# A second bank for q in the projection of an attention kernel, with the fourth score moved into the three score banks

## The chip, the cores and the metric

The kernel runs on one core of a Trainium2 chip. Its time is the device time of one launch in microseconds (us). Three runs of the kernel before took 796.98, 797.04 and 799.42 us; the median is 797.04 us.

## What is computed

One block of a transformer: x is (2, 512, 512), all in fp32. The part that the change touches is the attention's projection and its scores, cut here to what matters:

```
xn = layernorm(x)
q = rmsnorm((xn @ Wq.T) per head, q_norm_w)      # 32 heads of 128
k = rmsnorm((xn @ Wk.T) per head, k_norm_w)      # 8 heads of 128
v = (xn @ Wv.T) per head                         # 8 heads of 128
scores = q @ k.T / sqrt(128) + bias              # 4 q heads for each k head; causal, with slopes
attn = softmax(scores)
s = concat(attn @ v) @ Wo.T
g = silu(routed mixture of 8 rank-16 experts of xn)
out = x + s * g
```

## The kernel before, in words

The 1024 rows are 8 blocks of 128 (4 for each of 2 batches), and the 32 heads are 8 groups of 4 q heads with one k and one v head. One unit is one block of rows for one group: 64 units, numbered t. A unit of block i in its batch has i + 1 key blocks (`keys_of`), so 1, 2, 3, 4, 1, 2, 3, 4 over the 8 units of a group. Every fp32 product is made of three matmuls of split values, high x high, high x low and low x high (`three`, L1149 to L1153).

The five engines each run a list of their own, written out by hand, and meet by semaphores. In the steady part each list is a loop over slots (`slot`, once for each engine), 59 slots in all. In slot t:

- TensorE (PE) makes the scores of unit t, four heads; adds the output product of unit t - 3 (`out`); mixes the values of unit t - 2 (`mix`); and projects unit t + 3 (`project`): 4 chunks of the 512 input channels, and in each chunk 3 matmuls of 512 columns for q into one PSUM bank and 3 of 256 columns for k and v into a second (`qkv_ps`).
- VectorE (DVE) adds the bias to the scores (`bias`), sums the squares of q and k of unit t + 2 (`square_sums`), makes the low part of v, takes reciprocals, normalizes q and k of t + 2 in one instruction of 640 elements (`normalize_qk`, L963), transposes them in 32x32 squares (`square_both`), adds the output of t - 3, makes the low parts of q and k of t + 1 (`turned_qk_lo`), transposes the probabilities of t (`square_probs`) and makes the low part of the mix of t - 2 (`mixed_lo`).
- ScalarE (ACT) squares q and k of t + 2 in one instruction (`square_qk`, L678), copies v, takes the exponentials of t, then the high parts of q and k of t + 1 (`turned_qk_hi`, L664), scales the probabilities of t, and copies the moved probabilities of t - 1 (`moved_hi`, L691).
- GpSimd (POOL) makes the inverse root of the sums: an add of epsilon, a power and a product (`inverse_rms`, L517, L519, L523), and then the low parts of the moved probabilities of t - 1 (`turned_lo`, L529, one for each key block).
- The sync engine (SP) issues the transfers that finish the transposes through memory (`move`): 4 writes of the squared q and k of t + 2, 8 writes of the squared probabilities of t, 1 read of q and k, 2 reads of probabilities.

What holds the projection: the matmuls of unit t + 3 overwrite the two banks of `qkv_ps`, so they wait until v's low part and the normalization of unit t + 2 have read them:

```
if t > 0:
    pe.wait_ge(qk_norm_ready, ONE(g, t - 1, 1))
    pe.wait_ge(v_lo_ready, ONE(g, t - 1, 1))
```

Scores: heads 0, 1 and 2 go to three banks of `score_ps`, and from unit 3 on head 3 goes to `turn_ps`, so that PE writes all four scores of a unit without waiting for one of its biases (`score_bank`, `has_own_bank`). The bias of a head waits for its own score, except heads 2 and 3 together, and in units of 1 or 2 key blocks heads 0 and 1 together.

Memory: `squares` holds ACT's squares and then, under another name (`qk_squared`), the transposed q and k that SP's writes read. So ACT's squares of a unit wait for the writes of the unit before to have landed (`qk_written`, in `square_qk`).

Once in 8 slots (t = 5 of 8) the next group's projection weights are split as well, on ACT, DVE and POOL, and once (t = 2 of 8) the output weights, on ACT and POOL.

## Time and profile before

| | |
|---|---|
| median of three runs | 797.04 us |
| the profiled execution | 793.71 us |
| its span, first to last instruction | 791.6 us |
| mean granted TensorE clock over the span | 0.983 of full speed |
| busy: PE, PE weight load | 727.6 us (92%), 612.6 us (77%) |
| busy: DVE, ACT, POOL | 583.8 (74%), 559.6 (71%), 399.9 us (51%) |

Busy shares are means over stages. PE's matmuls overlap one another in the record (each lasts longer than the time to the next one's start), so PE's work is best read from start to start. What a wait costs is read where it stands: a gap in PE's row of starts is lost; a gap of another engine only where PE waits for it later.

### The profile page before, as it was taken

Reading aid. Unit: us, or ns where it says so; the run is one execution under the profiler, and the core shown is the slowest. Engines: PE = TensorE matmul, PEld = TensorE weight load, DVE = VectorE, ACT = ScalarE, POOL = GpSimd, SP = SyncE. Lnnn points to the kernel's source line nnn. Section 1 sums busy time; section 2 is a strip of 40 time slices with the busy share of each in tenths; the row PEclk is TensorE's granted clock in tenths of the full one; section 3 lists DMA queues with packets and bytes.
Section 4 is the critical chain, followed back from the end, with each engine's and each line's share of the span. In section 5 each row is a group of like instructions: output and inputs, shape, how many; then the busy total and the mean of one; then the engine's idle time right before and its main releaser. Section 6 shows DMA issues by size and latency. Waiting matters only on the chain.

```text
span 791.6 us, 14475 instructions
## 1 busy us (share of the span) xinstructions
PE 727.6 (92%) x3729; PEld 612.6 (77%) x3729; DVE 583.8 (74%) x1378; ACT 559.6 (71%) x1370; POOL 399.9 (51%) x423
## 2 busy tenths in 40 slices
PE   8888989999899999999899989999899998999697
PEld 7777867778788778887778778887787787787575
DVE  7855778677886778687877769778786778777555
ACT  4664767686676877777777876777686866768863
POOL 5313373555444762544644664445635554447347
PEclk9999999999999999999999999999999999999989
DMA  7014848678495767859485765858477784956642
GB/s 285 1 28 115 270 107 237 191 214 239 109 275 156 223 185 194 240 145 294 130 236 169 231 201 151 270 153 258 130 224 205 208 251 109 268 159 188 187 148 94
DMA packets 214772, 148.01 MB, mean 187 GB/s; under 512 B 48992, under 2 KB 205536, under 8 KB 214624
## 3 DMA queue, kind: packets, MB, share of 16 engines
q1 hardware_dynamic: 214752, 147.77, 64.7%
q8 instruction: 9, 0.15, 0.1%
q14 instruction: 11, 0.09, 0.0%
HBM read 85.84 MB, written 61.87 MB: 187 GB/s over the span
## 4 chain that ended last, share of the span: by engine, by line
PE 33%; issue 26%; POOL 24%; DVE 10%; ACT 4%; DMA 2%; POOLq 1%; SPq 1%; DVEq 0%; ACTq 0%
POOL pt_lo L529 10%; POOL inv_rms L519 8%; PE qkv_ps L1151 7%; PE qkv_ps L1152 6%; PE qkv_ps L1153 6%; POOL wo_lo L511 3%; DVE qk_norm L963 3%; DVE sums L947 2%; PE score_ps L1151 2%; PE score_ps L1153 2%; POOL sums_eps L517 2%; PE score_ps L1152 2%; PE out_ps L1151 2%; PE out_ps L1152 2%; PE out_ps L1153 2%
## 5 line engine op out<-in xcount | busy, mean ns | idle before, releaser
L529 POOL TENSOR_TENSOR pt_lo<-x_sb,pt_hi 128x512 fp32r<-128x512 f32 x153 | 195.3, 1303 | 240.8 <-ACT pt_hi L691 240.8
L1151 PE MATMUL qkv_ps<-w_hi,xt_hi 128*128 128x512 f32 (+1 forms) x512 | 182.0, 355 | 40.4 <-DVE qk_norm L963 38.4
L1152 PE MATMUL qkv_ps<-w_lo,xt_hi 128*128 128x512 f32 (+1 forms) x512 | 176.9, 345 | 0.0
L1153 PE MATMUL qkv_ps<-w_hi,xt_lo 128*128 128x512 f32 (+1 forms) x512 | 175.8, 343 | 0.0
L639 ACT ACTIVATE probs<-probs,neg_max 128x128 f32<-128x128 f32 (+3 forms) x256 | 141.7, 556 | 37.4 <-DVE neg_max L899 35.0
L1151 PEld LDWEIGHTS qkv_ps<-w_hi,xt_hi 128*128 128x128 f32 x512 | 99.2, 194 | 70.2 <-DVE qk_norm L963 34.6
L899 DVE CUSTOM_DVE_ANT_0 probs<-score_ps,cst,slope 128x128 f32<-128x128 f32 (+3 forms) x196 | 102.0, 545 | 54.1 <-PE score_ps L1153 46.1
L647 ACT ACTIVATE probs<-probs,recip 128x128 f32<-128x128 f32 (+3 forms) x252 | 122.2, 549 | 6.1 <-DVE recip L906 6.0
L918 DVE STREAM_TRANSPOSE squared<-probs 128x256 f32<-128x256 f32 (+3 forms) x124 | 99.7, 823 | 18.9 <-ACT probs L647 17.0
L1152 PEld LDWEIGHTS qkv_ps<-w_lo,xt_hi 128*128 128x128 f32 x512 | 99.6, 195 | 11.9
L1153 PEld LDWEIGHTS qkv_ps<-w_hi,xt_lo 128*128 128x128 f32 x512 | 99.2, 194 | 12.0
L963 DVE TENSOR_TENSOR qk_norm<-qkv_ps,inv 128x640 f32<-128x640 f32 x64 | 52.6, 822 | 71.5 <-POOL inv L523 71.5
L1151 PE MATMUL out_ps<-wo_hi,o_hi 128*128 128x512 f32 x252 | 100.4, 398 | 3.9 <-DVE o_lo L941 3.8
L1152 PE MATMUL out_ps<-wo_lo,o_hi 128*128 128x512 f32 x252 | 98.8, 392 | 0.0
L1153 PE MATMUL out_ps<-wo_hi,o_lo 128*128 128x512 f32 x252 | 98.7, 392 | 0.0
L691 ACT ACTIVATE pt_hi<-x_sb 128x512 fp32r<-128x512 f32 x153 | 86.0, 619 | 13.9 <-DMA x_sb<-turning 13.8
L678 ACT ACTIVATE squares<-qkv_ps 128x640 f32<-128x640 f32 x64 | 44.7, 698 | 65.0 <-PE qkv_ps L1153 54.4
L519 POOL TENSOR_TENSOR inv_rms<-sums_eps,minus_half 128x5 f32<-128x5 f32 x64 | 78.5, 1227 | 5.0
L664 ACT ACTIVATE q_hi<-qk_moved 128x512 fp32r<-128x512 f32 x45 | 28.4, 630 | 68.0 <-DMA qk_moved<-turning_qk 68.0
L947 DVE TENSOR_REDUCE sums<-squares 128x5 f32<-128x640 f32 x64 | 52.3, 818 | 22.0 <-ACT squares L678 21.7
L1151 PE MATMUL mix_ps<-pt_hi,v_hi 128*128 128x512 f32 x160 | 62.6, 391 | 0.0
L1153 PE MATMUL mix_ps<-pt_hi,v_lo 128*128 128x512 f32 x160 | 62.3, 389 | 0.0
(166 smaller groups left out, 1444.7 us busy)
## 6 DMA issues: line engine op xcount, KB each, us to landing
turning_qk<-squares SPq DMA_DIRECT2D x240, 80.0 KB, 1.9
qk_moved<-turning_qk SPq DMA_DIRECT2D x60, 320.0 KB, 3.2
turning<-squared SPq DMA_DIRECT2D x120, 128.0 KB, 2.2
x_sb<-turning SPq DMA_DIRECT2D x30, 512.0 KB, 5.0
w_raw<-wqkv SPq DMA_DIRECT2D x32, 384.0 KB, 5.3
turning<-squared SPq DMA_DIRECT2D x120, 96.0 KB, 1.9
x_sb<-turning SPq DMA_DIRECT2D x30, 384.0 KB, 4.2
turning<-squared SPq DMA_DIRECT2D x128, 64.0 KB, 1.8
```

The costliest lines, as they stand in the source:

```text
L519: nc.gpsimd.tensor_tensor(inv_rms[:, :], sums_eps[:, :], minus_half[:, 0:NORMED], ALU.pow).then_inc(inv_rms_ready, 1)
L529: nc.gpsimd.tensor_tensor(by_quad(pt_lo, j), moved_block(t, j), by_quad(pt_hi, j).bitcast(F32), ALU.subtract).then_inc(pt_lo_by_pool, 1)
L639: nc.scalar.activation(probs[:, h, 0:n], probs[:, h, 0:n], ACT.Exp, bias=neg_max[:, h:h + 1], scale=-1.0, accum_out=total[:, h:h + 1]).the ...
L647: nc.scalar.activation(to[:, h, 0:n], probs[:, h, 0:n], ACT.Copy, scale=recip[:, h:h + 1]).then_inc(probs_ready, 1)
L691: nc.scalar.activation(by_quad(pt_hi, j), moved_block(t, j), ACT.Copy).then_inc(pt_hi_ready, 1)
L899: nc.vector.tensor_tensor_reduce(probs[:, h, 0:n], score_bank(t, h, at_end), cst[:, C_DIST + SEQ - n:C_DIST + SEQ], slope[:, h:h + 1], HUG ...
L918: nc.vector.transpose(blocks[:, :, 0:keys_of(t), :, :], probs[:, h:h + 2, 0:n].rearrange("p h (j k n) -> p h j k n", k=QUADS, n=QUAD)).the ...
L947: nc.vector.tensor_reduce(sums[:, :], squares[:, :].rearrange("p (h d) -> p h d", h=NORMED), AX.X, ALU.add).then_inc(sums_ready, 1)
L963: nc.vector.tensor_tensor(qk_norm[:, :, :], qkv_flat[:, 0:QK].rearrange("p (h d) -> p h d", h=NORMED), inv[:, :].unsqueeze(2).broadcast_to ...
L1151: pe.matmul(out, a_hi, b_hi, start=start, stop=False)
L1152: pe.matmul(out, a_hi, b_lo, start=False, stop=False)
L1153: return pe.matmul(out, a_lo, b_hi, start=False, stop=stop)
```

## The change

- The projection's q has two banks by turns, from unit 6 on (`two_banks`): `turn_ps` for even units and the first bank of `qkv_ps` for odd ones. q's 12 matmuls come before the 12 of k and v. q waits for the normalization of q of two units before (`q_norm_ready`), k and v for that of k of the unit before and for v's low part. Where the weights are new (block 0 of a group) the order is q, q, kv, kv of the first two chunks, then q, kv, q, kv.
- Head 3's score gives up `turn_ps`. In units of 1 or 2 key blocks it takes the free half of the third score bank. In units of 3 or 4 key blocks it takes head 0's bank, and waits for head 0's bias.
- The biases wait by twos in all units from 3 on: head 0's waits for the scores of heads 0 and 1.
- ACT squares q (512 elements) and k (128) by two instructions, DVE normalizes k (128) and q (512) by two; the reciprocals of heads 2 and 3 come between them.
- The normalized q and k now lie in the memory of the squares, and the transposed ones in memory of their own. So ACT's squares wait for DVE's transpose of the unit before, and DVE's transpose waits for the writes of the unit before.
- Each row of squares has one more element, which holds the epsilon, so the sum has it in and POOL's add is gone.

The diff, its core:

```
+        squares = sb("squares", [NORMED, HD + 1])
+        qk_norm = squares[:, :, 0:HD]
-        qk_squared = squares[:, :].rearrange("p (k n) -> p k n", k=QUADS)
+        qk_squared = sb("qk_squared", [QUADS, NORMED * QUAD])
...
+        def q_ps(u):
+            return turn_ps[:, :] if two_banks(u) and u % 2 == 0 else qkv_ps[:, 0, :]
+        def two_banks(u):
+            return u >= BY_TURN + 2
...
-        def score_bank(t, h, at_end=False):
+        def score_bank(t, h):
             n = keys_of(t) * P
-            if h == 3 and has_own_bank(t, at_end):
-                return turn_ps[:, 0:n]
+            if h == 3 and has_half(t):
+                return score_ps[:, 2, SEQ // 2:SEQ // 2 + n]
             return score_ps[:, h % (3 if t >= 2 else 2), 0:n]
+        def has_half(t):
+            return t >= 2 and keys_of(t) <= 2
...
 POOL, inverse_rms
-                nc.gpsimd.tensor_tensor(sums_eps[:, :], sums[:, :], eps_sum[:, :], ALU.add).then_inc(eps_added, 1)
-                pool.wait_ge(eps_added, ONE(g, u, 1))
...
 ACT, square_qk
-                act.wait_ge(qkv_ready, ONE(g, u, 1))
-                if u > BY_TURN:
-                    act.wait_ge(qk_written, QK_WRITTEN(g, u - BY_TURN, 0))
-                nc.scalar.activation(squares[:, :], qkv_flat[:, 0:QK],
+                act.wait_ge(q_ready, ONE(g, u, 1))
+                if 0 < u <= BY_TURN:
+                    act.wait_ge(qk_turned, TWO(g, u, 0))
+                elif u > BY_TURN:
+                    act.wait_ge(qk_squared_ready, ONE(g, u - BY_TURN, 0))
+                nc.scalar.activation(squares[:, 0:HPG, 0:HD], q_ps(u).rearrange("p (h d) -> p h d", h=HPG),
                                      ACT.Square).then_inc(squares_ready, 1)
+                act.wait_ge(kv_ready, ONE(g, u, 1))
+                nc.scalar.activation(squares[:, HPG, 0:HD], k_ps, ACT.Square).then_inc(squares_ready, 1)
...
 DVE, bias
-                by_twos = t > 2 and not at_end and (h >= 2 or keys_of(t) <= 2)
+                by_twos = t > 2 and not at_end
...
 DVE, square_both
-                dve.wait_ge(qk_norm_ready, ONE(g, u, 1))
+                dve.wait_ge(q_norm_ready, ONE(g, u, 1))
+                if u > BY_TURN:
+                    dve.wait_ge(qk_written, QK_WRITTEN(g, u - BY_TURN, 0))
...
 DVE, slot
-                    normalize_qk(g, t + 2)
+                    normalize_k(g, t + 2)
...
                     reciprocals(g, t, 2)
                 if here(t + 2, left):
+                    normalize_q(g, t + 2)
                     square_both(g, t + 2)
...
 PE, project_q and project_kv
+                if c == 0:
+                    if two_banks(t):
+                        pe.wait_ge(q_norm_ready, ONE(g, t - 2, 1))
+                    elif t > 0:
+                        pe.wait_ge(q_norm_ready, ONE(g, t - 1, 1))
...
+                if c == 0 and t > 0:
+                    pe.wait_ge(k_norm_ready, ONE(g, t - 1, 1))
+                    pe.wait_ge(v_lo_ready, ONE(g, t - 1, 1))
...
+                if two_banks(t) and t % BLOCKS > 0:
+                    for c in chunks:
+                        project_q(g, t, c)
+                    for c in chunks:
+                        project_kv(g, t, c)
...
 PE, scores
-                elif h == 3 and not has_own_bank(t, at_end):
+                elif h == 3 and not has_half(t):
                     pe.wait_ge(biased_ready, PER_HEAD(g, t, 1))
```

How the rows stand now. PE, the end of the scores of a unit of 4 key blocks, before and then in the change (`score_ps` are the three score banks, `turn_ps` the bank that head 3 had; in brackets the semaphores waited for):

```order
L1151 MATMUL score_ps<-k_hi,q_hi 128x512
L1152 MATMUL score_ps<-k_lo,q_hi 128x512
L1153 MATMUL score_ps<-k_hi,q_lo 128x512
L1151 MATMUL turn_ps<-k_hi,q_hi 128x512
L1152 MATMUL turn_ps<-k_lo,q_hi 128x512
L1153 MATMUL turn_ps<-k_hi,q_lo 128x512
L1308 ISA
L1312 ISA [waits acc_ready,o_lo_ready]
```

```order
L1170 MATMUL score_ps<-k_hi,q_hi 128x512
L1171 MATMUL score_ps<-k_lo,q_hi 128x512
L1172 MATMUL score_ps<-k_hi,q_lo 128x512
L1303 REGISTER_ALU
L1170 MATMUL score_ps<-k_hi,q_hi 128x512 [waits biased_ready]
L1171 MATMUL score_ps<-k_lo,q_hi 128x512
L1172 MATMUL score_ps<-k_hi,q_lo 128x512
L1358 ISA
L1362 ISA [waits acc_ready,o_lo_ready]
```

Head 3 had no wait, and now has one for head 0's bias in the middle of the scores.

PE, the start of the projection in the same slot, before and then in the change:

```order
L1161 REGISTER_ALU
L1151 MATMUL qkv_ps<-w_hi,xt_hi 128x512 [waits v_lo_ready,qk_norm_ready]
L1152 MATMUL qkv_ps<-w_lo,xt_hi 128x512
L1153 MATMUL qkv_ps<-w_hi,xt_lo 128x512
L1151 MATMUL qkv_ps<-w_hi,xt_hi 128x256
L1152 MATMUL qkv_ps<-w_lo,xt_hi 128x256
```

```order
L1180 REGISTER_ALU
L1170 MATMUL turn_ps<-w_hi,xt_hi 128x512 [waits q_norm_ready]
L1171 MATMUL turn_ps<-w_lo,xt_hi 128x512
...
L1200 REGISTER_ALU
L1170 MATMUL qkv_ps<-w_hi,xt_hi 128x256 [waits v_lo_ready,k_norm_ready]
L1171 MATMUL qkv_ps<-w_lo,xt_hi 128x256
L1172 MATMUL qkv_ps<-w_hi,xt_lo 128x256
```

The wait for the unit before has moved behind q's 12 matmuls; in front of them stands a wait for the unit two before.

DVE, from v's low part to the transpose of q and k in one slot, before and then in the change (`squares` is now also the name of the memory of the normalized q and k):

```order
L953 TENSOR_TENSOR v_lo<-qkv_ps,v_hi 128x128 [waits v_hi_ready]
L906 RECIPROCAL recip<-total 128x2 [waits exp_ready]
L963 TENSOR_TENSOR qk_norm<-qkv_ps,inv 128x640 [waits qk_squared_ready,inv_ready]
L906 RECIPROCAL recip<-total 128x2 [waits exp_ready]
L969 STREAM_TRANSPOSE squares<-qk_norm 128x5x4x32 [waits qk_norm_ready]
```

```order
L964 TENSOR_TENSOR v_lo<-qkv_ps,v_hi 128x128 [waits v_hi_ready]
L915 RECIPROCAL recip<-total 128x2 [waits exp_ready]
L969 TENSOR_TENSOR squares<-qkv_ps,inv 128x128 [waits inv_ready]
L915 RECIPROCAL recip<-total 128x2 [waits exp_ready]
L974 TENSOR_TENSOR squares<-turn_ps,inv 128x4x128
L982 REGISTER_ALU [waits q_norm_ready]
L983 STREAM_TRANSPOSE qk_squared<-squares 128x5x4x32 [waits qk_written]
```

k is normalized first, by itself; q's normalization comes after the second reciprocal, and the wait for the writes stands at the transpose.

## Rows read from the trace of the kernel before

**Rows 1.** The page: busy time of each engine.

```profile
PE 727.6 (92%) x3729; PEld 612.6 (77%) x3729; DVE 583.8 (74%) x1378; ACT 559.6 (71%) x1370; POOL 399.9 (51%) x423
```

**Rows 2.** Waits: who waited for whom, us in total, times, longest.

```profile
DVE qk_norm L963 <- POOL inv L523: 71.5, 55, 2.6
ACT q_hi L664 <- DMA qk_moved<-turning_qk: 68.0, 36, 3.5
ACT squares L678 <- PE qkv_ps L1153: 54.4, 24, 5.5
...
PE qkv_ps L1151 <- DVE qk_norm L963: 38.4, 29, 3.0
...
ACT squares L678 <- DMA turning_qk<-squares: 10.0, 11, 2.0
```

**Rows 3.** Windows, projections alone: stretch, its length, PE busy, granted clock, DMA.

```profile
107.46:113.30 5.84, 5.84 (x24) 0.71 0.23 56
...
656.62:661.22 4.60, 4.45 (x24) 1.00 0.29 71
541.13:545.43 4.30, 4.30 (x24) 1.00 0.71 221
```

**Rows 4.** Windows, one group of 8 slots: length, busy PE, PEld, DVE, ACT, POOL, clock.

```profile
463.90:555.30 91.40, 86.48 (x438) 72.80 (x437) 70.03 (x162) 67.26 (x166) 47.76 (x50) 0.98 0.70 200
```

**Rows 5.** Timeline of PE: start, duration, what, idle before it and releaser.

```profile
107.46 0.49 PE L1151 MATMUL qkv_ps<-w_hi,xt_hi 128*128 128x512 f32 x1 [2.96 <-DVE qk_norm L963]
```

**Rows 6.** Timeline of PE, scores of 4 key blocks: the first matmuls of heads 2, 3.

```profile
399.05 0.39 PE L1151 MATMUL score_ps<-k_hi,q_hi 128*128 128x512 f32 x1
...
399.73 0.39 PE L1151 MATMUL turn_ps<-k_hi,q_hi 128*128 128x512 f32 x1
```

**Rows 7.** Timeline of DVE: head 0's bias in the same unit.

```profile
398.81 0.73 DVE L899 CUSTOM_DVE_ANT_0 probs<-score_ps,cst,slope 128x512 f32<-128x512 f32 x1
```

**Rows 8.** Timeline, the same slot: from one transfer of q and k to the next.

```profile
404.23 0.63 ACT L664 ACTIVATE x_sb<-qk_moved 128x512 f32<-128x512 f32 x1 [1.05 <-DMA qk_moved<-turning_qk]
...
406.79 2.47 DVE L918 STREAM_TRANSPOSE squared<-probs 128x1024 f32<-128x1024 f32 x2 [0.96 <-ACT probs L647]
...
415.81 0.63 ACT L664 ACTIVATE q_hi<-qk_moved 128x512 fp32r<-128x512 f32 x1 [2.08 <-DMA qk_moved<-turning_qk]
```

**Rows 9.** Timeline of ACT: squares of 640 elements, then v's high part of 128.

```profile
377.36 0.71 ACT L678 ACTIVATE squares<-qkv_ps 128x640 f32<-128x640 f32 x1 [1.65 <-DMA turning_qk<-squares]
377.96 0.27 ACT L683 ACTIVATE v_hi<-qkv_ps 128x128 fp32r<-128x128 f32 x1
378.11 0.85 ACT L594 ACTIVATE w_hi<-w_raw 128x768 fp32r<-128x768 f32 x1
```

**Rows 10.** Timeline of ACT: 512 elements from PSUM, and what starts behind them.

```profile
352.00 0.57 ACT L653 ACTIVATE o_hi<-mix_ps 128x512 fp32r<-128x512 f32 x1
352.48 1.14 ACT L691 ACTIVATE pt_hi<-x_sb 128x512 fp32r<-128x512 f32 x2
```

**Rows 11.** Timeline of DVE: 128, 640 and 512 elements from PSUM, each with its successor.

```profile
345.28 0.29 DVE L953 TENSOR_TENSOR v_lo<-qkv_ps,v_hi 128x128 fp32r<-128x128 f32 x1
345.48 0.16 DVE L906 RECIPROCAL recip<-total 128x2 f32<-128x2 f32 x1
346.12 0.82 DVE L963 TENSOR_TENSOR qk_norm<-qkv_ps,inv 128x640 f32<-128x640 f32 x1 [0.48 <-POOL inv L523]
346.86 0.15 DVE L906 RECIPROCAL recip<-total 128x2 f32<-128x2 f32 x1
...
347.74 0.65 DVE L988 TENSOR_TENSOR acc<-out_ps,acc 128x512 f32<-128x512 f32 x1
348.32 0.67 DVE L929 TENSOR_TENSOR q_lo<-qk_moved,q_hi 128x512 fp32r<-128x512 f32 x1
```

**Rows 12.** Lines by form, POOL: epsilon's add, mean ns in front of the bar's idle time.

```profile
L517 POOL TENSOR_TENSOR sums_eps<-sums,eps_sum 128x5 f32<-128x5 f32 x64 | 17.2, 269 | 87.4 <-DVE sums L947 87.4
```

**Rows 13.** Timeline of POOL: the same add beside DVE's split of the weights.

```profile
469.79 0.93 POOL L517 TENSOR_TENSOR sums_eps<-sums,eps_sum 128x5 f32<-128x5 f32 x1
```

More of the change, by code:

```diff
@@ L944, in square_sums @@
             def square_sums(g, u):
[L946 to L947 removed]
+                dve.wait_ge(squares_ready, TWO(g, u, 2))
+                if u == 0:
+                    dve.wait_ge(eps_set, 1)
+                nc.vector.tensor_reduce(sums[:, :], squares[:, :, :], AX.X, ALU.add).then_inc(sums_ready, 1)
             def value_lo(g, u):
@@ L1177, in project @@
-                if KC - 1 in chunks:
-                    last.then_inc(qkv_ready, 1)
+                if t == 0:
+                    pe.wait_ge(w_lo_done, c + 1)
+                elif m == 0 and c < EARLY_W:
+                    pe.wait_ge(w_lo_by_dve, (g + t // BLOCKS - 1) * EARLY_W + (c + 1))
+                elif m == 0:
+                    pe.wait_ge(w_lo_by_pool, (g + t // BLOCKS - 1) * (KC - EARLY_W) + (c - EARLY_W + 1))
+                last = three(q_ps(t), xt_hi[:, c, rows], xt_lo[:, c, rows], w_hi[:, c, 0:QW], w_lo[:, c, 0:QW], c == 0, c == KC - 1)
@@ new lines, in project_q, with project_kv @@
+                if c == KC - 1:
+                    last.then_inc(q_ready, 1)
+            def project_kv(g, t, c):
+                m = t % BLOCKS
+                rows = slice(m * P, (m + 1) * P)
+                if c == 0 and t > 0:
+                    pe.wait_ge(k_norm_ready, ONE(g, t - 1, 1))
+                    pe.wait_ge(v_lo_ready, ONE(g, t - 1, 1))
+                last = three(qkv_ps[:, 1, 0:QKV - QW], xt_hi[:, c, rows], xt_lo[:, c, rows],
+                             w_hi[:, c, QW:QKV], w_lo[:, c, QW:QKV], c == 0, c == KC - 1)
+                if m == BLOCKS - 1 and c < EARLY_W:
+                    last.then_inc(w_left, 1)
+                if c == KC - 1:
+                    last.then_inc(kv_ready, 1)
@@ L1346, in end @@
                 for h in range(3):
-                    scores(g, last, h, at_end=True)
+                    scores(g, last, h)
                 mix(g, before - 1, 1)
@@ L1350, in end @@
                     turn_probs(before, n)
-                scores(g, last, 3, at_end=True)
+                scores(g, last, 3)
                 out(g, before - 1)
```

97 lines of the change are left out of this document (45 added, 52 removed).

## The prediction

> **What bounds the kernel now.** I read the busy times first: PE is busy 92% of the span, so what it loses is small and has to be found place by place [rows 1]. The view of waits gives the place: PE waited 38.4 us in 29 pieces for DVE's normalization before a projection [rows 2]. The timeline of PE shows the worst kind, 2.96 us idle before the first matmul at 107.46 [rows 5]. Such a wait costs twice: that projection had a mean granted clock of 0.71 and took 5.84 us, against 4.30 us at clock 1.00 elsewhere [rows 3]; so PE ran a part of it at the lower of its two levels, 1.2 GHz instead of 2.4.
>
> But PE is not alone. ACT waited 68.0 us in 36 pieces for the transfer of q and k, DVE 71.5 us in 55 pieces for POOL's inverse, and ACT only 54.4 us in 24 pieces for PE's projection [rows 2]. So there is a second ring without PE in it: ACT takes q and k (404.23), scales the probabilities, DVE transposes them (406.79, 2.47 us), SP issues 8 writes and then the read of q and k, and ACT takes the next q and k on landing, at 415.81: 11.58 us for a slot of 4 key blocks, with a wait at both ends [rows 8]. A group of 8 slots takes 91.4 us, in which PE is busy 86.5 [rows 4]. The reader is to see two rings of nearly equal length; a change that shortens one is paid only as far as the other follows.
>
> **The change, part by part.** There are 59 steady slots, or 7.4 groups of 8.
>
> *q's second bank, kv behind q.* PE's wait now stands behind q's 12 matmuls, which are 12 x 0.228 = 2.7 us (three take 399.73 - 399.05 = 0.68 us [rows 6]), and needs only k's normalization, which ends some 0.5 us earlier than the joint one (0.20 against 0.74 us from start to start [rows 11]). The longest wait is 3.0 us [rows 2], so cover of 3.2 us swallows all of them. Of the 38.4 us about 3.6 lie in front of units below 6, which keep one bank; 34.8 go. Seven projections took longer than 4.5 us, the first and the last of them in [rows 3]; above 4.30 they cost 1.5 us each in four cases and 1.3, 0.3 and 0.3 us in the others, 8 us in all. PE's side: **-43 us** as a ceiling. What is late next is the first score of the next unit, which waits for q and k of the other ring.
>
> *Head 3 in head 0's bank.* It touches 30 slots, 15 of 4 and 15 of 3 key blocks. Head 3 would start 0.68 us after head 2 [rows 6]. It now waits for head 0's bias: this starts when head 1's last matmul is out, 399.05 + 0.16 (the record's 0.39 less the 0.23 to the next start), plus about 0.2 for the signal, takes 0.73 [rows 7], and about 0.2 for its accumulator and the way back: 400.3 against 399.73, so 0.6 us. If DVE comes late, by the 0.3 us that a longer queue before the bias easily gives, 0.9. Bounds: 30 x 0.6 = 18 and 30 x 0.9 = 27 us; nothing below, since no row lets the bias end before head 2's matmuls. I take 0.67, **+20 us**, near the lower end, because in [rows 7] DVE begins its bias at 398.81, before the second score is out. Queued behind that wait on PE: the output, the mix and the projection. PE's side nets -23.
>
> *Biases by twos.* DVE's first bias waits for head 1 as well, 0.68 us later. It costs where DVE waits for PE; it is inside the 0.6 above. The exponentials behind it have ACT's later wait for q and k as cover (1.9 us on the mean, 68.0 / 36 [rows 2]); without that cover it would be 0.68 us a slot.
>
> *Two squares and two normalizations for one each.* By starts: ACT's 640 elements hold it 0.60 us, 128 hold it 0.15 [rows 9], 512 hold it 0.48 [rows 10], so +0.03. DVE: 0.74, 0.20 and 0.58 [rows 11], so +0.04. With 59 slots: **+4 us** in the second ring. q's squares can start before k and v are projected, which is worth up to 0.45 us in the slots where ACT waits for PE, 24 of 64 [rows 2]: **-7 us** at 0.3 each.
> By durations the split would cost more: 0.57 + 0.27 - 0.71 on ACT [rows 9, 10] and 0.65 + 0.29 - 0.82 on DVE [rows 11], together 0.25 us a slot, 15 us in all. The Trainium skill (VectorE: DVE Perf Modes, "The TRN2 errata") gives a fixed part for each instruction that reads PSUM, 172 cycles on ScalarE and 120 on VectorE; from it I estimate 0.27 us a slot, 16 us in all, as the durations have it and unlike the starts. I go by the starts, because the next instruction of the same engine does begin before the record of the one before it ends [rows 9, 11].
>
> *The squares' memory.* ACT's wait for the writes, 10.0 us in 11 pieces [rows 2], goes; DVE's transpose, which comes later, gets it, with about 4 us more room in between. **-10 us** in the second ring as a ceiling, nothing as a floor (where ACT only reaches its next wait sooner); I take 8.
>
> *POOL's add.* 0.27 us on the mean [rows 12], in the path where DVE waits for the inverse (55 of 64 slots [rows 2]), but in the ring of ACT and the transfers only where the normalization holds DVE's transposes, which I put at 3 slots in 8: 0.27 x 22 = **-6 us**. Beside the weights' split it took 0.93 us [rows 13]; the mean has this in it, and I add nothing for it.
> The Trainium skill (SBUF — State Buffer, "shared port pair") says that a GpSimd instruction that reads SBUF and a VectorE one with two SBUF inputs exclude one another for their whole length. By that the power takes over the add's 0.7 us of blocking, and the sum gets nothing extra from those 7 slots; counting the 0.93 as saved would give 5 us more.
>
> **The sum.** PE's ring: -43 + 20 = -23. Second ring: +4 - 7 - 8 - 6 = -17, of which I take off 1 for the reciprocals that now stand in front of q's normalization. Both must be shorter for the time to be; the lesser is 16. The profiled execution took 793.7 us and so comes to 777.7; the median is 3.3 above it, and 797.0 - 16 gives **781 us**. From no change one can tell here about 0.3%, 2.4 us.
>
> **The rivals.**
> 1. *PE leads and the second ring follows* (its waits were only idle time before a late PE). For it: 24 waits of ACT for PE [rows 2]. Against it: q and k arrive late in more slots. Then PE's side with head 3 at its lower bound is paid, -43 + 18 = -25: 772 us.
> 2. *The second ring doesn't shorten.* If the split instructions cost their durations, 15 instead of 4 us, the ring gives -17 + 11 = -6: 791 us, and with the wait for the writes moved rather than gone, -6 + 8 = +2: 799. PE's waits would then stand at the first score or the output instead of the projection. This holds too if the second bank does not do what it says. For it: ACT and DVE are busy 71% and 74% of the span with waits in every slot [rows 1, 2]. Against it: the starts of [rows 9 to 11]. Centre 793.
> 3. *Slower: head 3's wait.* Place: PE, in the middle of the scores of units with 3 or 4 key blocks. DVE does its transposes (2.47 us for 4 key blocks [rows 8]) and the mix's low part before the first bias. If PE, with its waits gone, comes to the scores that much earlier, head 3 waits for all of DVE's arrears: up to 2.1 us for 4 key blocks and 1.1 for 3, which is 15 x 3.2 = 48 us against the 43 won; with the +4 of the splits 797 + 9 = 806. It decides from 43 / 30 = 1.4 us a slot on. For it: DVE had no idle time before the bias in [rows 7]. Against it: it was not late there.
>
> **How the numbers follow.** The forecast has 0.52, rival 1 0.13, rival 2 0.19 (half of it below 794.6 and half within 0.3%), rival 3 0.16. Faster is 0.52 + 0.13 + 0.09 = 0.74, the same 0.10, slower 0.16. The range goes from 768 (rival 1 with 4 us for the bound of the other terms) to 799 (the end of rival 2), and leaves rival 3 out.
>
> **What would show it.** PE's wait for a normalization before a projection under 5 us in total, and no projection at a clock below 0.9 behind one; a new wait of head 3's score for a bias, 30 times, 12 to 27 us by the view of waits; ACT's wait for the writes gone, and DVE's transpose without one; ACT's wait for the transfer of q and k as large as now or larger; waits of PE at the first score for the low part of k. The forecast is wrong if head 3's waits are over 1.4 us each, if ACT's wait for q and k shrinks while PE has none (rival 1), or if a group of 8 slots still takes 91 us (rival 2).

## The result, and the profile of the changed kernel

The changed kernel takes **823.3 us** (median of 4, 819.8 to 826.1) against 797.0 for the kernel before in the same session: ratio 1.030, interval 1.026 to 1.033, slower. The prediction was 781 us with a range of 768 to 799; the time lies outside it, on the other side. The profiled execution took 819.8 us. Here and below medians are of all runs, and ratios with their 95% intervals are of the runs in the faster of the chip's two states.

The page of the changed kernel, span and busy times, then the two queues that fetch instructions (packets, MB, share of 16 engines):

```profile
span 818.0 us, 14522 instructions
...
PE 736.7 (90%) x3729; PEld 617.1 (75%) x3729; DVE 604.2 (74%) x1442; ACT 562.8 (69%) x1434; POOL 388.5 (47%) x359
...
q14 instruction: 42, 0.34, 0.1%
q8 instruction: 9, 0.15, 0.1%
```

PE is busy 9 us longer than in [rows 1] and idle 17 us longer. The q14 line is new. The kernel before had the line below; packets and bytes of the other queues are the same in both.

```profile
q14 instruction: 11, 0.09, 0.0%
```

The waits of the changed kernel (who waited for whom: us in total, times, longest), to be held against [rows 2]:

```profile
ACT probs L643 <- DVE neg_max L908: 88.2, 88, 3.3
ACT q_hi L668 <- DMA qk_moved<-turning_qk: 80.3, 36, 3.8
...
DVE squares L969 <- POOL inv L527: 47.8, 46, 2.4
PE score_ps L1170 <- DVE neg_max L908: 42.6, 29, 5.3
...
DVE probs L908 <- issue: 24.4, 13, 5.7
...
PE score_ps L1170 <- DVE k_lo L942: 15.4, 11, 7.7
...
PE qkv_ps L1170 <- DVE squares L974: 3.4, 2, 2.4
```

Much of what the prediction said one would see is there: the wait before the projection fell from 38.4 to 3.4 us, ACT's wait for the writes is gone, its wait for q and k grew from 68.0 to 80.3, PE waits at the first score for the low part of k. Three things are not as foreseen. A group of 8 slots takes 95.5 us, not less than 91 (columns as in [rows 4]), which is the prediction's own sign for a second ring that does not shorten:

```profile
462.30:557.80 95.50, 87.55 (x436) 73.18 (x436) 72.70 (x171) 67.72 (x174) 46.28 (x43) 0.98 0.68 192
```

Head 3's wait is 42.6 us, and DVE stands idle for 24.4 us with no releaser at all ("issue"). The timeline of DVE and PE shows that the last two meet at the first slot of a pass of the loop (start, duration, what, idle time before it):

```profile
363.55 0.69 DVE L950 TENSOR_TENSOR o_lo<-mix_ps,o_hi 128x512 fp32r<-128x512 f32 x1 [0.45 <-ACT o_hi L657]
367.04 0.75 DVE L908 CUSTOM_DVE_ANT_0 probs<-score_ps,cst,slope 128x512 f32<-128x512 f32 x1 [2.81 <-issue]
```

```profile
361.57 0.39 PE L1170 MATMUL score_ps<-k_hi,q_hi 128*128 128x512 f32 x1
...
367.86 0.80 PE L1170 MATMUL score_ps<-k_hi,q_hi 128*128 128x512 f32 x1 [4.76 <-DVE neg_max L908]
368.45 0.63 PE L1171 MATMUL score_ps<-k_lo,q_hi 128*128 128x512 f32 x1
```

The scores that the bias needs were out by 362.2 (the first line of PE is head 1's first matmul), DVE was free at 364.2, and its bias began at 367.0. PE waited 4.76 us in the middle of the scores and then ran matmuls of 0.63 us instead of 0.39. This comes back six times, once in each later pass of 8 slots, with 2.7 to 2.9 us of DVE's idle time and a wait of 4.6 to 5.3 us on PE each. In the other slots head 3's wait is 0.4 to 0.7 us, but for one of 1.2 and one of 1.7. Of the 24.4 us another 5.7 stand once, ahead of the loop.

### The profile page after: what moved, and what is told of

The parts are those of the page before. It is cut to its first block, busy times and chain, and to the rows that moved or that the text cites. A ratio compares the mean times of both kernels' runs of the same rounds, so it can differ in the third digit from the quotient of the medians.

```text
span 818.0 us, 14522 instructions
## 1 busy us (share of the span) xinstructions
PE 736.7 (90%) x3729; PEld 617.1 (75%) x3729; DVE 604.2 (74%) x1442; ACT 562.8 (69%) x1434; POOL 388.5 (47%) x359
## 4 chain that ended last, share of the span: by engine, by line
issue 33%; POOL 13%; DVE 11%; DMA 10%; ACT 9%; SPq 9%; PE 7%; DVEq 0%; ACTq 0%; POOLq 0%
SPq L433 9%; DMA qk_moved<-turning_qk 8%; POOL pt_lo L533 7%; POOL inv_rms L523 5%; ACT probs L651 4%; DVE squared L927 3%; DVE k_lo L942 2%; DVE probs L908 1%; DVE q_lo L938 1%; ACT wo_hi L608 1%; ACT probs L643 1%; DVE sums L958 1%; POOL inv L527 1%; DMA w_raw<-wqkv 1%; PE score_ps L1170 1%
## 5 line engine op out<-in xcount | busy, mean ns | idle before, releaser
L908 DVE CUSTOM_DVE_ANT_0 probs<-score_ps,cst,slope 128x128 f32<-128x128 f32 (+3 forms) x256 | 130.0, 544 | 71.1 <-PE score_ps L1172 32.9
L1170 PE MATMUL qkv_ps<-w_hi,xt_hi 128*128 128x256 f32 (+1 forms) x396 | 128.6, 325 | 5.4 <-DVE squares L974 3.4
L1171 PE MATMUL qkv_ps<-w_lo,xt_hi 128*128 128x256 f32 (+1 forms) x396 | 127.9, 323 | 0.0
L1172 PE MATMUL qkv_ps<-w_hi,xt_lo 128*128 128x256 f32 (+1 forms) x396 | 127.4, 322 | 0.0
L523 POOL TENSOR_TENSOR inv_rms<-sums,minus_half 128x5 f32<-128x5 f32 x64 | 78.5, 1227 | 98.8 <-DVE sums L958 98.8
L1170 PE MATMUL score_ps<-k_hi,q_hi 128*128 128x256 f32 (+2 forms) x192 | 71.6, 373 | 58.2 <-DVE neg_max L908 42.6
L1170 PEld LDWEIGHTS score_ps<-k_hi,q_hi 128*128 128x128 f32 x192 | 37.1, 193 | 73.9 <-DVE neg_max L908 53.9
L668 ACT ACTIVATE q_hi<-qk_moved 128x512 fp32r<-128x512 f32 x45 | 28.4, 631 | 80.3 <-DMA qk_moved<-turning_qk 80.3
L1171 PE MATMUL score_ps<-k_lo,q_hi 128*128 128x256 f32 (+2 forms) x192 | 66.8, 348 | 0.0
L1172 PE MATMUL score_ps<-k_hi,q_lo 128*128 128x256 f32 (+2 forms) x192 | 66.8, 348 | 0.0
L958 DVE TENSOR_REDUCE sums<-squares 128x5 f32<-128x645 f32 x64 | 52.6, 822 | 15.4 <-ACT squares L688 15.3
```

Source lines behind the costliest of these rows:

```text
L523: nc.gpsimd.tensor_tensor(inv_rms[:, :], sums[:, :], minus_half[:, 0:NORMED], ALU.pow).then_inc(inv_rms_ready, 1)
L908: nc.vector.tensor_tensor_reduce(probs[:, h, 0:n], score_bank(t, h), cst[:, C_DIST + SEQ - n:C_DIST + SEQ], slope[:, h:h + 1], HUGE, ALU.a ...
L958: nc.vector.tensor_reduce(sums[:, :], squares[:, :, :], AX.X, ALU.add).then_inc(sums_ready, 1)
L1170: pe.matmul(out, a_hi, b_hi, start=start, stop=False)
L1171: pe.matmul(out, a_hi, b_lo, start=False, stop=False)
L1172: return pe.matmul(out, a_lo, b_hi, start=False, stop=stop)
```

## The experiments

**Theories.** *Code position:* the change added instructions on VectorE; its loop now ends at instruction 394 of its program instead of 382 and has passed the edge of a block of instruction memory. *Theory 1:* head 3's wait and the split pieces are slow by themselves, on TensorE's path. *Theory 2:* the second ring, through SyncE and the transfers, sets the slot, and PE only waits elsewhere. *Theory 3:* the second bank does give time, and the split pieces take it back. Ratios are to the kernel before in the same session (797.3 to 800.2 us).

### Position in the code

```
# 1 and 2, kernel before, DVE, ahead of its loop (n = 12, 4)
+            for _ in range(n):
+                dve.engine_nop()
```

> The kernel before with 12 empty instructions on VectorE in front of its loop, so that the loop ends at instruction 394 of VectorE's program, where the changed kernel's loop ends, instead of 382. Nothing else differs. Theory (code position): the loop's last instructions have passed the edge of a block of instruction memory, so that each jump back to the loop's start waits for code: VectorE idles 2 to 4 us with no releaser at the start of each of its 6 or 7 later loop passes, TensorE waits there, and the time is 820 to 840 us, with some 40 packets in the instruction queue instead of 11. Rival (head 3's wait and the split pieces are slow by themselves): 12 empty instructions of about 0.06 us cost under 1 us once, 797 to 798 us, 11 packets.

> The kernel before with 4 empty instructions on VectorE in front of its loop: the loop ends at 386. Theory (code position): either the edge is not passed yet and the time stays 797 us, or it is passed and the time is 820 to 840 as with 12; nothing between. Rival: 797 us.

With 12 empty instructions the kernel before takes **819.1 us** (1.027, 1.022 to 1.032), with 4 of them 797.8 (0.999, 0.996 to 1.003). The page and the waits of the run with 12:

```profile
q14 instruction: 42, 0.34, 0.2%
```

```profile
DVE probs L899 <- issue: 17.1, 6, 3.2
...
DVE sums L947 <- issue: 10.7, 6, 2.1
```

Twice in each later pass DVE stands for code, about 2.9 and 1.8 us on the mean. PE pays before the projection, where it waits 56.7 us for the normalization instead of 38.4. The 31 further packets carry 0.25 MB. So 21 us hang on where a loop lies.

The Trainium skill (Runtime: NRT & Kernel Launch, "Instruction fetch mechanics") says that code is fetched in blocks of 256 instructions, that two blocks are held, fetched in sequence, and that a taken branch out of them stalls. The trace agrees on the extra fetches at each jump back. That two blocks are held it does not show: this loop, of some 240 to 250 instructions, touches only two blocks and stalls all the same.

```
# 3, changed kernel: 244 x dve.engine_nop() behind VectorE's first memsets
# 4, changed kernel, "trimmed"
-            normalize_k(0, 0)
-            normalize_q(0, 0)
+            normalize_qk(0, 0)                 # units 0 to 3
...
+            with dve.Fori(0, GROUPS - 1) as g:
+                for t in range(3, BLOCKS + 3):
+                    tail(g, t - 1, GROUPS)     # square_probs x2, mixed_lo
+                    slot(g, t, GROUPS)
...
```

> The changed kernel with 244 empty instructions on VectorE at the front of its program: the loop's body, itself unchanged, stands at 393 to 638 and so within one block of 256 instructions again if the edge lies between 382 and 394. Theory (code position): the idle time without a releaser at the loop's start goes (6 times 2.7 to 2.9 us), TensorE's wait for head 3's bank in the first slot of a pass falls from about 5 to about 1 us, one group of heads takes 88 to 90 us instead of 95, and the time is 823 - 38 plus what 244 empty instructions cost at the front, up to 15 us: 785 to 800. Rival: the waits in the first slot stay at 5 us, 823 plus 5 to 15 us: 828 to 838.

> The changed kernel with 9 instructions fewer on VectorE ahead of the loop's end: the first four units are normalized by one instruction each, the loop is turned so that the transposes of the probabilities and the subtraction of the slot before stand at its top, the first memsets are joined or on POOL, and the first square signals nothing of its own. The loop is at 140 to 385. Theory (code position): if the edge lies at 385 or later (the second run tells: it holds for 386), the time is 779 to 790 us, and the loop's start shows no idle time without a releaser; if it lies at 382 to 384, the time stays 818 to 826. Rival: 820 to 826 whatever the edge, since the score banks' waits are unchanged.

Both take the stall away (13 and 11 packets), by moving the same loop or by shortening what stands before it. The first measured 824.2 us, outside both of its forecasts. It has 8.4 us of idle time at its front, where the empty instructions stand, and the 5.7 once ahead of the loop, which the changed kernel has too and the trimmed one has not; since they stay when the code moves by 244 instructions, they do not hang on this edge. Its later passes take 93.2 us on the mean (from jump to jump of VectorE), those of the trimmed kernel 93.4, those of the changed kernel 95.0; so in the steady part the two agree, and 8.4 + 5.7 us cover what they differ by. The trimmed kernel takes **812.8 us** (1.020, 1.014 to 1.026) against 823.3: 10 us of the changed kernel's 26 are code position, 8 by the ratios. The forecast 779 to 790 was wrong: 15 us remain. Its waits on PE:

```profile
PE score_ps L1182 <- DVE neg_max L909: 22.4, 29, 2.1
PE score_ps L1182 <- DVE k_lo L943: 15.9, 11, 7.7
PE turn_ps L1182 <- POOL w_lo L508: 5.3, 12, 0.5
```

and a group of 8 slots (its columns as in [rows 4]):

```profile
472.00:565.00 93.00, 87.31 (x443) 72.62 (x442) 72.57 (x171) 67.48 (x174) 47.02 (x42) 1.00 0.69 195
```

Head 3's wait is now 22.4 us in 29 pieces. That looks like the predicted 20 (bounds 18 to 27), but it is made of two things. 21 of the waits are 0.4 us on the mean, 8.3 us together. The other 8 are 1.2 to 2.1 us, 14.1 us together, seven of them at the same slot of a group, and DVE has no idle time without a releaser there. Here is one, from the trimmed kernel's timeline:

```profile
357.28 0.98 DVE L928 STREAM_TRANSPOSE squared<-probs 128x768 f32<-128x768 f32 x1 [1.08 <-ACT probs L653]
358.70 0.69 DVE L951 TENSOR_TENSOR o_lo<-mix_ps,o_hi 128x512 fp32r<-128x512 f32 x1 [0.44 <-ACT o_hi L659]
359.31 0.74 DVE L909 CUSTOM_DVE_ANT_0 probs<-score_ps,cst,slope 128x512 f32<-128x512 f32 x1
360.11 0.50 PE L1182 MATMUL score_ps<-k_hi,q_hi 128*128 128x512 f32 x1 [1.77 <-DVE neg_max L909]
```

PE had come early, and DVE still had the transpose and the low part of the mix of the slot before to do: the mechanism of the prediction's rival 3, in one slot of eight. Of the changed kernel's waits of 4.6 to 5.3 us some 2.8 are the code, and about 2 are this.

All runs below are built on this one or on the kernel before, and all but the eighth show 11 or 12 packets.

### The parts one by one

> The kernel before with the change's score part alone: head 3 takes head 0's bank (a half of head 2's bank for one or two key blocks) and all biases wait by twos; one bank for q, joint normalization, the add on POOL and the shared memory as before. VectorE's loop ends at 378. Theory 1 (head 3's wait is a price on TensorE's path): TensorE's waits at the first score matmul of head 3 come in as 22 us in 29 places, as in the trimmed changed kernel, its waits before the projection stay above 30 us, and the time is 810 to 820. Theory 2 (a ring through VectorE and ScalarE sets the slot, TensorE only waits elsewhere): the projection's waits fall from 38 by about what head 3's waits add, 797 to 803.

> The kernel before with the eps as a column of the squares (POOL's add is gone, some 0.3 us of 1.2 in each unit), the normalization in the squares' memory and the turned squares in memory of their own; joint normalization, banks and biases as before. VectorE's loop ends at 384. My terms for these parts, 6 us for the add and 0 to 8 for the memory: 783 to 793, with TensorE's wait before the projection at 25 to 32 instead of 38. Rival (the inverse is not on the path that sets the slot): 796 to 799, and VectorE waits as before.

```
# 5, kernel before: score part alone
-            if h == 3 and has_own_bank(t, at_end):
-                return turn_ps[:, 0:n]
+            if h == 3 and has_half(t):
+                return score_ps[:, 2, SEQ // 2:SEQ // 2 + n]
# 6, kernel before: epsilon as a column of squares, no add on POOL,
#    norms in the squares' memory, qk_squared apart
```

The score part takes 802.5 us (1.007, 1.005 to 1.009), the memory part 800.8 (1.002, 0.999 to 1.005). In the first, the waits are

```profile
PE qkv_ps L1151 <- DVE qk_norm L963: 30.4, 24, 2.8
PE score_ps L1151 <- DVE neg_max L899: 11.6, 29, 0.6
```

so head 3 brings 11.6 us (0.4 a slot) and the projection gives 8 of it back: theory 2 for this part. The 14 us that the prediction had for the memory and the add did not come. The two together:

> The kernel before with the score part and the memory part of the change together (head 3 in head 0's bank, biases by twos, no add on POOL, the normalization in the squares' memory), joint squares and joint normalization, one bank for q. VectorE's loop ends at 380. Against the run of the trimmed kernel without the second bank (824) only the split pieces, q's and k/v's matmuls in that order, and the trimming are missing. If the split is what costs (theory 3): 801 to 809, the sum of the two parts alone (5 and 3 us). If the two parts cost more together than apart: 815 to 826.

801.7 us against 800.2 (1.002, 1.000 to 1.005). These parts are nearly free.

> The trimmed changed kernel with head 3's score matmuls on TensorE behind the first head's three output matmuls (0.7 us) instead of ahead of them, so that the wait for head 0's bias has something in front of it. Theory 1: the waits for head 0's bias fall from 22 to under 5 us, and the time from 813 to 793 to 800. Theory 2 (the ring sets the slot, and head 3's scores now come up to 0.7 us later for VectorE): 810 to 820, and the waits come back at the projection or at the first score.

```
# 7, PE, trimmed kernel
+                    for h in range(3):
+                        scores(g, t, h)
+                if here(t - 3, left):
+                    out(g, t - 3, range(0, 1))
+                if here(t, left):
+                    scores(g, t, 3)
+                if here(t - 3, left):
+                    out(g, t - 3, range(1, HPG))
```

812.7 us: no change. Head 3's wait is gone from the list, and this stands in its place:

```profile
PE out_ps L1182 <- DVE o_lo L951: 17.1, 20, 1.8
...
PE out_ps L1182 <- POOL wo_lo L519: 11.7, 6, 2.3
```

Taking 22 us of waits from PE gave nothing, and they came back at the output. That fits theory 2, by which PE's path is not what sets the time while all transfers are in place. It does not prove it, since the edit also gives VectorE head 3's scores up to 0.7 us later.

> The trimmed changed kernel with the score banks of before (head 3 in its own bank, the biases of heads 0 and 1 apart for three and four key blocks) and one bank for q; what is left of the change is k and q normalized and squared apart, q's matmuls in front of k's and v's by chunks, and the squares' memory. VectorE's loop ends at 389: whether the edge is passed shows in the instruction queue (11 packets or about 42). Theory 1: without head 3's wait and without the second bank the split pieces cost 1 to 4 us net of the memory's gain: 795 to 802. Theory 2 (the split itself, 0.29 and 0.68 us in place of 0.82 and 0.25 us more on ScalarE, lengthens the ring): 808 to 815. With 42 packets 10 to 20 us more in either.

> The trimmed changed kernel without the second bank for q (every unit's q in the first bank); the score banks, the biases by twos, the split normalization and squares, q's matmuls in front of k's and v's chunk by chunk and the squares' memory as in the change. VectorE's loop ends at 385. If the second bank gives nothing because a ring through SyncE and the transfers sets the slot (theory 2): 811 to 818, no more than 4 us from the 813 with it, and TensorE's waits before the projection are back at 25 to 40 us. If the second bank does give time and the split pieces take it away again (theory 3): 825 to 845.

```
# 12, trimmed kernel (8: also the score banks of before)
         def two_banks(u):
-            return u >= BY_TURN + 2
+            return False
```

The eighth shows 42 packets and so says nothing on the split (829.3 us); with the second it puts the edge between 386 and 389. The twelfth takes 823.9 us (814.9 to 828.1; 1.027, 1.019 to 1.035). The forecasts were 811 to 818 without a worth of the bank and 825 to 845 with one, and the time lies between. The second bank thus gives about 11 us by the medians and 5 by the ratios, and the intervals overlap (1.019 to 1.026). Against the run with joint squares below, whose interval lies clear of the trimmed kernel's, it is 9 by the ratios: a gain, of a size that stays open. What is left, 20 to 25 us over the run with the score and memory parts, lies in the split, the order of q's and k/v's matmuls and the trimming; the two runs that follow tell them apart.

> The trimmed changed kernel without the second bank, with q's and k's squares in one instruction (0.70 us, instead of 0.59 and 0.27), k and q still normalized apart. If the second square, 0.15 us later for the sums, is the larger part of the split's price: 808 to 816. If it is the split normalization (q's end comes behind a reciprocal, and TensorE's next q waits for it): 818 to 826.

> The trimmed changed kernel without the second bank, with q's normalization directly behind k's, ahead of the second reciprocal (0.15 us) instead of behind it; nothing else differs from the run without the second bank (824). From the start of the first normalization to the end of the last it took 1.18 us a unit there against 0.82 in the kernel before. If that end is what the split costs on the projection's path: 1.18 falls by 0.1 to 0.2 us, and the time by 6 to 14 us, to 810 to 818. If the order of q's and k/v's matmuls or the trimming is what costs: 821 to 827.

```
# 17, ACT, on 12: one Square over 640 columns
# 18, DVE, on 12
                 if here(t + 2, left):
                     normalize_k(g, t + 2)
+                    normalize_q(g, t + 2)
                 if (t + 3) % BLOCKS == 0 and here(t + 3, left):
                     set_factor(g, t + 3)
                 if here(t, left):
                     reciprocals(g, t, 2)
                 if here(t + 2, left):
-                    normalize_q(g, t + 2)
                     square_both(g, t + 2)
```

Joint squares: 824.3 us (1.031, 1.028 to 1.034), so the second square costs nothing. q's normalization directly behind k's: **804.2 us** (1.006, 1.004 to 1.009), 20 us less for one instruction moved (16 to 20 by the ratios), more than the 6 to 14 expected. The order of the matmuls and the trimming are still in this run, so together with the two instructions they cost at most some 3 us over the score and memory parts. The timeline of VectorE shows why, first of the run without the second bank, then with the instruction moved:

```profile
393.91 0.29 DVE L976 TENSOR_TENSOR squares<-qkv_ps,inv 128x128 f32<-128x128 f32 x1 [1.06 <-POOL inv L529]
394.12 1.54 DVE L896 COPY factor<-cst 128x5 f32 x1
395.58 0.15 DVE L916 RECIPROCAL recip<-total 128x2 f32<-128x2 f32 x1
395.65 0.67 DVE L981 TENSOR_TENSOR squares<-qkv_ps,inv 128x512 f32<-128x512 f32 x1
```

```profile
387.43 0.29 DVE L976 TENSOR_TENSOR squares<-qkv_ps,inv 128x128 f32<-128x128 f32 x1 [1.06 <-POOL inv L529]
387.64 0.68 DVE L981 TENSOR_TENSOR squares<-qkv_ps,inv 128x512 f32<-128x512 f32 x1
388.24 0.96 DVE L896 COPY factor<-cst 128x5 f32 x1
```

The change had put not only the reciprocals of heads 2 and 3 in front of q's normalization, but in one slot of each group the copy of the factors too, which takes 1.54 us there. It began 0.29 us behind this on POOL, and in all seven groups it ended about 0.03 us after the first of the two instructions (393.83 to 395.63 here):

```profile
393.83 3.58 POOL L508 TENSOR_TENSOR w_lo<-w_raw,w_hi 128x768 fp32r<-128x768 f32 x2
```

From the start of the first normalization to the end of the last a unit takes 0.82 us before, 1.18 in the run without the bank and 0.89 with the instruction moved (means over 60 units of VectorE's timeline). Seven units of the 60, those with the copy, take 2.4 us each in the second. Times 60, 0.30 us are 18 us, near the 20 that were won, and more than half of them lie in the units with the copy. PE paid for it right away, at 396.45, and more in matmuls at the slower clock, of 0.63 us instead of 0.39:

```profile
396.45 0.79 PE L1182 MATMUL qkv_ps<-w_hi,xt_hi 128*128 128x512 f32 x1 [3.65 <-DVE squares L981]
397.03 0.63 PE L1183 MATMUL qkv_ps<-w_lo,xt_hi 128*128 128x512 f32 x1
```

PE's waits for q's normalization, without the second bank and then with the instruction moved:

```profile
PE qkv_ps L1182 <- DVE squares L981: 34.3, 20, 3.7
```

```profile
PE qkv_ps L1182 <- DVE squares L981: 22.7, 20, 2.2
```

They differ by 11.6 us. PE's busy time (744.2 and 739.4 us) and head 3's wait (15.7 and 11.3 us) add 9, which makes 21 us, against 19 between the two spans (821.6 and 802.4 us).

The slots also show what the second bank did. From ScalarE's copy of one unit's transferred q to that of the second unit after it, the pair of slots that begins with the copy of the factors takes 26.6 us without the bank, 24.5 with it (the trimmed kernel), 24.4 without it but with the instruction moved, and 24.2 in the run with the score and memory parts alone (means of five groups). So in these slots the bank and the moved instruction take away the same 2.2 us a group, 16 us in all: the bank mostly gave back what the late q had cost. That it gives anything beyond this no run shows.

### Transfers

> The kernel before with one step of SyncE's order moved: the read of the next unit's turned q and k is issued behind the first pair's four probability writes instead of behind all eight (a write's issue takes 0.46 us on SyncE, so 1.9 us earlier). Nothing is added or removed. Theory 2 (a ring sets the slot: q and k land, ScalarE's q_hi and k_hi and probabilities, VectorE's transpose of the probabilities, SyncE's writes and the next read, landing): ScalarE's wait for q and k falls from 68 to 10 to 40 us, TensorE's wait before the projection grows or stays, and the time is 770 to 790, since TensorE's 728 busy us stand next. Theory 1 (TensorE with the normalization sets it): 795 to 799, and ScalarE waits for something else.

> The trimmed changed kernel with the same step of SyncE's order moved. Theory 2: the second bank for q can now pay, so this gains more than the kernel before does from the same move: from 813 to 765 to 785, with TensorE's waits for the projection under 5 us and head 3's waits at 12 to 25. Theory 1: 808 to 815. If it gains only as much as the kernel before (20 us or less) and stays above it, head 3's wait and the split pieces cost more than the second bank gives even without the ring.

> The same with head 3's score matmuls behind the first head's output matmuls. Theory 2: with the ring loose, head 3's wait lies on TensorE's path, so hiding it is worth 5 to 20 us against the run before it, where it was worth nothing with the ring tight. If the ring still binds: no difference within 3 us.

```
# 9, 10 (11: also 7), SyncE, behind the first pair's writes instead of behind both
-                if u is not None:
-                    sp.wait_ge(qk_written, ...)
-                    sp.dma_start(qk_moved[:, :, :], ...)
+                    if u is not None and pair == 0:
+                        sp.wait_ge(qk_written, QK_WRITTEN(g, u - BY_TURN, 16 * QUADS))
+                        sp.dma_start(qk_moved[:, :, :], turning_qk[u % 2, ...])
```

The forecasts failed: 832.1 us from the kernel before, 817.2 from the trimmed one, 814.0 with head 3 late as well. Waits of ScalarE in the run from the kernel before:

```profile
ACT pt_hi L691 <- DMA x_sb<-turning: 74.0, 29, 6.1
...
ACT q_hi L664 <- DMA qk_moved<-turning_qk: 12.8, 16, 1.6
```

q and k were hardly waited for any more (68.0 us before), but the probabilities came late instead (13.8 before), since SyncE stood 47.9 us for the writes of q and k with the second pair's writes behind it. The move bought one transfer with another. With this order the trimmed kernel is the faster of the two, by 15 us (11 by the ratios), but both are slower than the kernel before.

> The kernel before with half of what is turned through DRAM left out: of the probabilities and of q and k only two of four quarters are written and read back (so the other half of their turned values is stale), which takes half of SyncE's issues (0.46 us each) and half of the bytes out of the slot. Theory 2 (transfers and their issue set the slot): 745 to 785, ScalarE's waits for q and k under 20 us, and TensorE's waits for the normalization stay or grow. Theory 1: 790 to 799.

> The trimmed changed kernel with the same half of the turned values left out. Theory 2: with the transfers out of the way the second bank pays, and this is 5 to 25 us faster than the kernel before with half of its moves, while with all moves it is 15 us slower. Theory 3 (head 3's wait and the split pieces cost more than the second bank gives under any transfers): slower than it by 5 to 20 us.

> The same with head 3's score matmuls behind the first head's output matmuls. If head 3's wait lies on TensorE's path once the transfers are out of the way: 5 to 20 us faster than the run before it. Otherwise within 3 us of it.

```
# 13 to 15, SyncE: both writes and both reads
-                    for q in range(QUADS):
+                    for q in range(HALF):
```

With half of the turned values left out the kernel before takes **748.9 us** (0.937, 0.934 to 0.941), the trimmed one 759.7, and 754.4 with head 3 late. So the transfers and their issue hold 48 us of the kernel before: theory 2's ring is real. PE is then busy 96% of the span, and its wait before the projection is

```profile
PE qkv_ps L1153 <- DVE qk_norm L965: 13.3, 16, 2.4
```

Theory 2 had expected this wait to stay or to grow. It fell from 38.4 us with nothing changed on PE or VectorE, so 25 us of what the second bank was to win were waits that the transfers had caused further up. The second bank has little left to win here; the trimmed kernel is 11 us slower than the kernel before, as theory 3 had it, and now, unlike with all transfers, hiding head 3's wait is worth 5 us.

## Why the prediction was wrong

**q's second bank, -43 as a ceiling, -23 paid after head 3.** The mechanism was right in part: the waits before the projection went. The granted clock of the profiled run did not rise, 0.975 against 0.983 before, and 0.985 in the trimmed kernel. The worth was wrong: 5 to 11 us against a run in which q is late, and by the slots above mostly a repair of that lateness. 25 of the 38.4 us were the transfers' doing (run 13). The prediction did name the other ring and took the lesser of two sums; but the gains that it gave the second ring did not come (below), and of the waits that were taken from PE a part came back at k's low part (15.9 us against 6.8 before) and the weights' low part (5.3 against 0.6).

**Head 3 in head 0's bank, +20.** As a sum the wait was near (22.4 us in the trimmed kernel), and that was in part luck. The plain wait is 0.4 us of idle time a slot, or nearly 0.6 from start to start, since a matmul's record lasts 0.16 us beyond the next one's start; so the 0.6 of the prediction's lower bound holds, though no row had shown its two terms of 0.2 us. The rest are eight long waits, for DVE's arrears. As a price it was 5 us alone and 2 with the memory part. A wait on PE is not a price when another ring sets the slot. Rival 3 wanted its arrears in every such slot; they came in one slot of eight, at 1.2 to 2.1 us. Its sign, over 1.4 us each, did come (42.6 us in 29 pieces), but only because DVE's waits for code stood on top.

**Split squares and normalizations, "+4 us", and 1 us for the reciprocals.** This is the step that failed most. The squares cost nothing, as costed by starts. The late end of q's normalization cost 16 to 20 us where q has one bank (runs 12 and 18): it went from 0.82 to 1.18 us behind the start of the first. The prediction costed the two instructions (+0.04) and put 1 us for the reciprocals in between, and did not list the copy of the factors, which the change had put there too and which takes 1.5 us beside POOL's split of the weights. The 15 or 16 us that the prediction set against the starts, from durations and from the fixed part in the Trainium skill (VectorE: DVE Perf Modes, "The TRN2 errata"), came nearer in size, but for another reason: with q directly behind k, two instructions end 0.07 us later than one, nearer to the +0.04 of the starts than to the +0.12 of the durations. What the late q costs with two banks was not measured by itself.

**The squares' memory -8, the add -6, q's squares earlier -7.** Memory and add together measured +1.5 us (interval -1 to +4). ACT's 10.0 us of waits for the writes went and gave no time. Its waits for PE before the squares fell from 54.4 to 21.6 us in the trimmed kernel, which no run has by itself. VectorE's gap from the end of the sums to the start of the normalization fell by only 0.12 us (2.64 to 2.52 in run 16), not 0.27, without the add. So the second ring, forecast 18 us shorter, did not shorten: a group takes 93.4 us in the trimmed kernel, 91.2 in the kernel before. That is the mechanism of rival 2, which had it end at 799 at most.

**What no step had.** The length of VectorE's loop. Nothing in the prediction counts instructions against the place of the code; the order of the changed kernel's instructions would have shown the loop's end move by 12. It is worth 8 to 10 us here, and 21 in the kernel before.

In sum, from the kernel before: score and memory parts +2, the split with q late about +22, the second bank -5 to -11, code position +8 to +10. The last two are uncertain by some 6 to 8 us to both sides, and the sum holds for this order of steps only, since the split's price and the bank's gain are in part the same time.

**Open.** The obvious kernel, second bank with q's normalization directly behind k's and the loop inside a block, was not run. If the gains of the bank and of the moved instruction added, it would come to about 793 to 799; the slots above speak against that, since both take away the same 2.2 us a group. So a time nearer to run 18's 804 is as likely, and no gain over the kernel before is to be expected from what was measured. Where the 15 us that the trimmed kernel keeps over the kernel before go, slot by slot, stays open too. No kernel that was run and does the whole computation beats the kernel before.

## What to carry to other kernels

Where an instruction is split, cost the end of the last piece, with everything that the new order lets in between, and not the pieces. A wait that vanishes from one engine is worth something only if this engine sets the slot; a run with something else taken away (half of the transfers, here) shows how much of the wait was that other thing's. And count the instructions of an engine's loop: when a change moves its end or start, look at the packets of the instruction queue before explaining any wait.

## What the runs showed of the hardware

- A loop of some 240 to 250 instructions on VectorE that ends at 389 or 394 of its program has 31 packets of code more over the run and stands 2.6 to 3.9 us once in each later pass, in the run with 12 empty instructions also 1.4 to 2.1 us a second time. One that ends at 386, or lies at 393 to 638, has no such stop in its passes. The edge lies between 386 and 389 of the kernel's own instructions.
- Empty instructions are not free: 244 of them at the front stood for 8.4 us.
- The copy of 5 columns takes 0.16 us alone and 1.0 to 1.6 us beside POOL's subtraction of the weights. It ended about 0.03 us after POOL's instruction in every group where it began beside one. The Trainium skill (SBUF — State Buffer, "shared port pair") says that the two engines arbitrate for one pair of ports, which the holder keeps for its full instruction while the other fully blocks, where VectorE's instruction has two SBUF inputs or runs in a mode with two ports. The trace agrees with these ends; whether this copy, with one input, ran in such a mode no run shows.
- SyncE needs 0.46 us for each of the transfers that it issues, where it does not wait (8 writes in 3.71 us, kernel before).
